# An adaLN transformer block: the LayerNorm chains of the pairs on GpSimd instead of VectorE and ScalarE, with new step orders

## The reference

```
h = layernorm(x) * (1 + ca) + sa
x = x + ga * attention(h)          # causal, softmax over |q k| / 16, then the product with Wo
h = layernorm(x) * (1 + cb) + sb
x = x + gb * ffn(h)
ffn: route each row: scores against 8 cluster and 64 tile signatures go through a
     piecewise linear curve, argmax cluster, argmax tile inside it; gelu/tanh compress to 2 numbers;
     the chosen tile's small spline gives a magnitude; y = h + magnitude * direction[tile] * scale;
     result = layernorm(y) * gamma + beta
```

## Time and profile before

| | |
|---|---|
| median of 3 runs | 475.73 us |
| profiled execution, its own time | 474.78 us |
| its span (first to last instruction) | 473.0 us |
| busy: PE, DVE, ACT, POOL | 403.7, 400.6, 295.5, 42.7 us |
| granted TensorE clock, mean | 0.939 |

### The profile page before, as it was taken

The page is one execution under the profiler, slowest core; times in us unless marked ns, Lnnn a source line. Parts: engine busy times, 40 slices in busy tenths (PEclk is TensorE's granted clock), DMA queues, the critical chain, the costliest instruction groups (busy, mean ns, idle before and its releaser), DMA issues.

```text
span 473.0 us, 7756 instructions
## 1 busy us (share of the span) xinstructions
PE 403.7 (85%) x2136; PEld 315.1 (67%) x2136; DVE 400.6 (85%) x1367; ACT 295.5 (62%) x645; POOL 42.7 (9%) x64
## 2 busy tenths in 40 slices
PE   2595799999999998999899989998999999963330
PEld 2563568767886886779586858786878787863330
DVE  4436536478799999999999999999999989998986
ACT  2230274949885968597758776797669865772410
POOL 2000003000000022001300040004000400040040
PEclk9879799999999999999999999999999999987565
DMA  8602102100300051104210320024101100110022
GB/s 303 148 2 79 48 1 62 41 11 2 100 2 33 8 161 46 34 2 135 77 35 1 122 91 35 1 59 154 24 1 49 65 24 1 67 46 0 0 90 89
DMA packets 26206, 26.59 MB, mean 56 GB/s; under 512 B 3874, under 2 KB 23588, under 8 KB 26164
## 3 DMA queue, kind: packets, MB, share of 16 engines
q1 hardware_dynamic: 24132, 24.25, 16.1%
q10 hardware_dynamic: 2032, 1.85, 1.2%
HBM read 17.66 MB, written 8.44 MB: 55 GB/s over the span
## 4 chain that ended last, share of the span: by engine, by line
DVE 51%; PE 32%; issue 9%; ACT 4%; ACTq 2%; DVEq 0%
PE bank L476 6%; PE bank L495 6%; PE bank L466 4%; PE bank L453 4%; PE bank L518 3%; DVE x L1043 3%; DVE res L1240 3%; DVE st L998 3%; DVE seg_val L1099 3%; DVE st L1206 3%; DVE val L1102 3%; DVE y L1230 3%; DVE v L1022 3%; DVE probs L1029 3%; DVE st L1049 2%
## 5 line engine op out<-in xcount | busy, mean ns | idle before, releaser
L476 PE MATMUL bank<-h,g 128*128 128x128 f32 (+3 forms) x256 | 80.6, 444 | 8.1 <-DVE v L1022 8.1
L495 PE MATMUL bank<-v,probsT 128*128 128x257 f32 x320 | 80.5, 383 | 0.0
L934 POOL TENSOR_TENSOR res<-x,gb_row 128x512 f32<-128x512 f32 x32 | 40.3, 1279 | 413.7 <-DMA out<-res 339.7
L466 PE MATMUL bank<-m_sb,h 128*128 128x258 f32 x256 | 66.0, 382 | 0.0
L476 PEld LDWEIGHTS bank<-h,g 128*128 128x128 f32 x256 | 44.5, 195 | 27.5 <-issue 11.0
L495 PEld LDWEIGHTS bank<-v,probsT 128*128 128x128 f32 x320 | 56.8, 190 | 8.0 <-issue 1.3
L453 PE MATMUL bank<-h,a_sb 128*128 128x512 f32 x128 | 59.8, 596 | 1.5 <-ACT gath L788 1.4
L466 PEld LDWEIGHTS bank<-m_sb,h 128*128 128x128 f32 x256 | 44.6, 192 | 6.8 <-issue 2.2
L699 ACT ACTIVATE bank<-bank,v 128x128 f32<-128x128 f32 (+1 forms) x64 | 31.6, 494 | 26.8 <-PE bank L476 23.8
L674 ACT ACTIVATE xhat<-x,nmr,rstd 128x256 f32<-128x256 f32 x64 | 36.7, 594 | 15.7 <-DVE nmr L989 15.7
L1029 DVE CUSTOM_DVE_ANT_0 probs<-bank,cmask 128x128 f32<-128x128 f32 (+1 forms) x64 | 31.1, 485 | 12.7 <-ACT bank L699 12.7
(11 more groups left out here) (175 smaller groups left out, 769.7 us busy)
## 6 DMA issues: line engine op xcount, KB each, us to landing
x<-in_L_attn_x SPq DMA_DIRECT2D x16, 512.0 KB, 3.8
out<-res SPq DMA_DIRECT2D x16, 512.0 KB, 3.0
gb_row<-gate_rows SPq DMA_DIRECT2D x16, 256.0 KB, 3.1
ga_row<-gate_rows SPq DMA_DIRECT2D x16, 128.0 KB, 2.9
wide<-in_L_wmod ACTq DMA_DIRECT2D x2, 768.0 KB, 7.3
res<-in_L_attn_Wq SPq DMA_DIRECT2D x1, 256.0 KB, 4.9
res<-in_L_attn_Wk SPq DMA_DIRECT2D x1, 256.0 KB, 7.2
res<-in_L_attn_Wo SPq DMA_DIRECT2D x1, 256.0 KB, 9.8
```

Of the source, the lines that this page charges most:

```text
L466: last = mm(ps[:, 0:VW], h[s][:, c, t * P:(t + 1) * P], m_sb[:, c, :], start=False, stop=(c == KC - 1))
L476: last = mm(ps[:, 0:w], g[s][:, c, t * P:(t + 1) * P], h[s][:, c, 0:w], start=(c == 0), stop=(c == KC - 1))
L495: last = mm(ps[:, 0:D + 1], probsT[s][t][:, j * P:(j + 1) * P], v_sb[s][:, j, 0:D + 1], start=(j == 0), stop=(j == t))
L934: gp.tensor_tensor(res[:, 2 * u:2 * u + 2, :], x2[p % 2][s][:, t, :], gb_row[p % 2][s][:, 1:2, :].broadcast_to([P, 2, D]), ALU.add).then_i ...
```

## The change

The three chains of the pairs go to GpSimd, as one step each: `a_ln`, `c_ln`, `y_ln`. The steps `a_var`, `a_nw`, `c_var`, `c_nw`, `y_var`, `y_nw` on DVE and `a_gs`, `c_gs`, `y_gs` on ACT are gone; the two halves of pair 0's LN1 in the setup stay as they were. The new chain has 14 operations, most of which wait for the one before; 1/sqrt is a `pow` with exponent -0.5, followed by a Newton step. `oa` now waits for the whole LN3 chain.

```diff
+            def layer_norm(chain, ln, ready):
+                ...
+                chain.mark(tt(dif, st[:, :, 1], st[:, :, 4], ALU.subtract))
+                chain.mark(tt(sums, st[:, :, 1], st[:, :, 4], ALU.add))
+                chain.link(pool, tt(var, st[:, :, 2], st[:, :, 5], ALU.add))
+                chain.mark(ts(var, var, 1.0 / D, EPS, ALU.mult, ALU.add))
+                chain.link(pool, tt(dif, dif, dif, ALU.mult))
+                chain.mark(ts(dif, dif, 0.25, None, ALU.mult))
+                chain.link(pool, ts(nmu, sums, -0.5, None, ALU.mult))
+                chain.link(pool, tt(var, var, dif, ALU.add))
+                chain.link(pool, tt(rstd, var, neg_half[:, :], ALU.pow))
+                chain.link(pool, tt(newt, rstd, rstd, ALU.mult))
+                chain.link(pool, tt(newt, newt, var, ALU.mult))
+                chain.link(pool, ts(newt, newt, -0.5, 1.5, ALU.mult, ALU.add))
+                chain.link(pool, tt(rstd, rstd, newt, ALU.mult))
+                tt(nmr, nmu, rstd, ALU.mult).then_inc(ready, 1)
+            @step
+            def a_ln(p):
+                pool_ln1.at(p - 1)
+                pool.wait_ge(st1_rdy, PT * p)
+                need(pool, xhat_ready, PT * p)
+                layer_norm(pool_ln1, ln1, ln1_ready)
+            @step
+            def c_ln(p):
+                pool.wait_ge(st2_rdy, PT * (p + 1))
+                ...
+            @step
+            def y_ln(p):
+                pool.wait_ge(st3_rdy, PT * (p + 1))
+                ...
             def superstep(k):
-                for i in range(0, 4):
-                    base(k, i)
-            for k in range(0, PAIRS + 0):
+                y_ln(k - 4)
+                base(k - 3, 0)
+                a_ln(k)
+                for i in range(1, 4):
+                    base(k - 3, i)
+                c_ln(k - 1)
+            for k in range(0, PAIRS + 4):
                 superstep(k)
...
             def oa(p, t):
                 if t == 0:
-                    dve_ln3.at(p)
-                    dve_ln3.wait(dve)
+                    dve.wait_ge(ln3_ready, p + 1)
```

More of the change, by code:

```diff
@@ L816, in _ @@
             first_half(1)
-            ahead.add(("a_gs", 0, ()))
             act.wait_ge(bias_rdy, 1)
@@ L1404, in superstep @@
-                a_st(k, 0, 3)
+                    y_st(k - 4, i)
+                b_ttr(k - 1, 0, 0)
+                for i in range(9, 12):
+                    loc(k - 3, i)
+                a_st(k, 0, 3)
+                a_st(k, 1, 0)
+                c_b2(k - 3)
+                for i in range(0, 2):
+                    lob(k - 3, i)
+                oa(k - 4, 0)
+                b_v(k - 1, 0, 1)
+                lob(k - 3, 2)
+                oa(k - 4, 1)
+                b_v(k - 1, 0, 2)
@@ new lines, in superstep @@
+                ob(k - 4, 5)
+                a_st(k, 1, 2)
+                b_ttr(k - 1, 0, 2)
+                oa(k - 4, 7)
+                ob(k - 4, 6)
+                b_v(k - 1, 1, 0)
+                ob(k - 4, 7)
+                clc(k - 2, 0)
+                a_st(k, 1, 3)
+                for i in range(1, 10):
+                    clc(k - 2, i)
+                spl(k - 3, 0)
+                b_ri(k - 1, 0, 0)
+                clc(k - 2, 10)
+                b_v(k - 1, 1, 1)
+                spl(k - 3, 1)
@@ new lines, in superstep @@
+                clc(k - 2, 11)
+                spl(k - 3, 2)
+                clb(k - 2, 0)
+                spl(k - 3, 3)
+                b_ttr(k - 1, 0, 3)
+                clb(k - 2, 1)
+                spl(k - 3, 4)
+                b_x2(k - 1, 0, 0)
+                clb(k - 2, 2)
+                spl(k - 3, 5)
+                b_v(k - 1, 1, 2)
+                clb(k - 2, 3)
+                y_(k - 3, 0)
+                clb(k - 2, 4)
+                y_(k - 3, 1)
+                b_ttr(k - 1, 1, 0)
@@ L1405, in superstep @@
+                pick(k - 2, 0)
+                y_st(k - 3, 0)
+                pick(k - 2, 1)
+                b_ttr(k - 1, 1, 1)
+                y_(k - 3, 2)
+                b_ri(k - 1, 0, 1)
+                b_x2(k - 1, 0, 1)
+                y_(k - 3, 3)
+                loc(k - 2, 0)
+                y_st(k - 3, 1)
+                loc(k - 2, 1)
+                b_ttr(k - 1, 1, 2)
                 y_(k - 3, 4)
-                y_st(k - 3, 0)
+                loc(k - 2, 2)
+                b_st(k - 1, 0, 0)
@@ L1468, in superstep @@
-                b_ttr(k - 1, 1, 0)
-                for i in range(7, 9):
-                    loc(k - 2, i)
-                b_ri(k - 1, 0, 1)
-                loc(k - 2, 9)
-                y_nw(k - 3, 1)
-                loc(k - 2, 10)
-                b_ttr(k - 1, 1, 1)
-                loc(k - 2, 11)
-                c_b2(k - 2)
-                lob(k - 2, 0)
+                loc(k - 2, 3)
+                b_v(k - 1, 1, 3)
+                y_st(k - 3, 2)
+                b_st(k - 1, 0, 1)
@@ new lines, in superstep @@
+                loc(k - 2, 4)
+                b_ri(k - 1, 0, 2)
+                b_x2(k - 1, 0, 2)
+                y_st(k - 3, 3)
+                loc(k - 2, 5)
+                y_st(k - 3, 4)
+                b_ttr(k - 1, 1, 3)
+                b_st(k - 1, 0, 2)
+                b_ri(k - 1, 0, 3)
+                b_ri(k - 1, 1, 0)
+                b_x2(k - 1, 0, 3)
+                b_st(k - 1, 0, 3)
+                b_ri(k - 1, 1, 1)
+                for i in range(0, 2):
+                    b_x2(k - 1, 1, i)
```

481 lines of the change are left out of this document (201 added, 280 removed), and 16 rows, old and new, of the table BANK.

## The result

The changed kernel took 575.18 us, median of 6 runs (574.19 to 579.35), against 475.0 us, median of 6 runs of the kernel before (measured again beside it): 1.2122 times as long, 95% interval [1.2082, 1.2163]. Forecast were 480.5 us, range 468 to 492. The direction was right and the size wrong by 95 us.

What follows compares the result with a forecast made beforehand. DVE was taken to bound the full pipeline, PE 2.7 us behind. Ramp -4.2, four periods -6.0, pair 7's step -2.1 and drain +18 made +5.7 us on the profiled execution's 474.78: 480.5 us, range 468 to 492.

Steps and rivals of the forecast that it cites:

- their term of the sum: Full pipeline: four periods, each going from 49.3 to 47.8 us, were to give -6.0 us.
- the match of 43.9 us: DVE work left in a full-pipeline period: 49.3 us less 3.3 of chain work and 2.1 of stall.
- The price of a chain: One norm's chain of 14 small operations on GpSimd: 3.5 us, with bounds of 2.2 and 17.5 us.
- rival 3: A dear chain: 6 us each on GpSimd, waited for twice per period, giving 508 us; chance 0.13.
- the prediction's own sign: Prediction wrong if drain is under 68 us, period at 46.6, or a GpSimd chain takes 5 us and more.
- a wait of 0.5 us: Full pipeline, LN3: DVE reaches oa at 7.6 us, y_ln ends at 8.1, so DVE waits 0.5 us.
- a wait of 2.0 us on DVE: Full pipeline, LN1: spl needs c_ga, held on ACT behind a_xh and a_ln, so DVE waits 2.0 us.
- PE's work per pair doesn't change: TensorE's work in each pair was to stay at 46.6 us, the floor of the period.
- The ramp: Start to last b_x2 of pair 2: reordered PE work 3.2 us and earlier first scores about 1 us, -4.2 us.
- pair 7's step: Step of pair 7, without a_st: 44.0 us with stalls against 46.1 before, -2.1 us.
- the drain: Last b_x2 to the end: +18 us, from more DVE work left, chain waits and bases.
- 1.8 + 1.4 + 3.5 = 6.7: Drain: DVE's waits before oa for y_ln, two of 1.8 and 1.4 us and the last of 3.5.

Runs made afterwards that it cites:

- e7: Kernel before with one line added: the first two GpSimd bases of a pair also wait for the second send; 466.2 us, 0.980 of before.
- e5: Changed kernel with each GpSimd chain cut from 14 operations to three, all new orders kept; 481.7 us.
- e10: Changed kernel with ScalarE's first c_xh moved behind b_g, b_abs and first GELUs, and first a_xh behind b_pt, c_ga and b_g; 528.5 us.
- e13: Kernel before with bases later and all three norms' chains on GpSimd (third's -mean on VectorE), second norm's ahead of the bases; 476.5 us.

## Why the prediction was wrong

- **What bounds the kernel before: right.** DVE with a stall of 2.1 us beside GpSimd's bases, PE 2.7 us behind. e7 removed that stall alone and the period fell by 2.0 us to 47.2. (The mean of the four periods is 49.15 us and not 49.3, so their term of the sum is -5.4 and not -6.0.)
- **What the change takes away: right in size, and the match of 43.9 us partly luck.** DVE is busy 44.0 to 44.3 us in a period. But the 43.9 are 5.4 taken from the period of 49.3; taken from DVE's busy 47.9 us they leave 42.5, to which the prediction adds 2.5 of stalls beside GpSimd (0.9 - 0.3 + 1.2 + 0.7). Like set against like, 45.0 were forecast.
- **The price of a chain: the first term that was mis-sized.** 3.5 us were taken, 5.1 to 6.5 measured. A link is 0.28 us and not 0.23; the pow 1.67 us, for which I had allowed a few tenths; and up to 1.5 us of meeting wide DVE operations. The bounds of 2.2 and 17.5 us held it, but rival 3, which says "6 us", had a chance of 0.13 only. The nearest row by size, a memset, says nothing of a pow. By the prediction's own sign, a chain of 5 us and more, it is refuted.
- **The waits: the step that failed.** The prediction has "a wait of 0.5 us" for LN3, "a wait of 2.0 us on DVE" for LN1 and none for LN2. For LN2 I missed that `c_ln`'s reader is ACT: `c_xh(k-1,0)` in front of `b_g(k,0,1)` is in the new ACT order and PE hangs on `b_g`. It cost 4.0 us of ACT and 3.3 of PE per period. For LN1 I saw that ACT holds `b_pt` and `c_ga` behind `a_xh`, but priced what DVE waits, 2.0 us, where 4.7 were measured, and not that PE hangs on `b_pt`, 5.0 us. The wait of 0.5 for LN3 did not come in the full pipeline. That rival 3 gave 508 us with about the right chain and two waits a period tells the same: even at the true length the waits, with the clock behind them, were 67 us short. e5 is the converse: with chains of 0.66 us, where the missed wait vanishes, the kernel takes 481.7 us.
- **"PE's work per pair doesn't change": failed.** Its matmuls don't, its time does: 47.1 to 52.9 us, since in most periods a stretch of 6.8 us at half clock begins behind the one idle and another within the other. The earlier trace rows has the granted clock at 1.00 in the full pipeline and 0.65 in the drain, so the column was there to read. The prediction holds no term for it; by the estimate above it was worth nearly half of what a period grew.
- **The parts of the sum.** The ramp: forecast -4.2, measured +29.4; four periods: -6.0, measured +46.3; pair 7's step: -2.1, measured +6.7; the drain: +18, measured +21.7 (79.2 us against the 75.5 that were worked out). Only the drain came near, and that was partly luck. DVE waits for a chain three times in it:

```profile
509.84 0.48 DVE L1254 SCALAR_TENSOR_TENSOR y<-y,nmu,gb_row 128x256 f32<-128x256 f32 x1 [6.09 <-POOL nmr L971]
...
542.21 0.48 DVE L1254 SCALAR_TENSOR_TENSOR y<-y,nmu,gb_row 128x256 f32<-128x256 f32 x1 [3.10 <-POOL nmr L971]
...
567.23 0.88 DVE L1254 SCALAR_TENSOR_TENSOR y<-y,nmu,gb_row 128x256 f32<-128x256 f32 x2 [5.17 <-POOL nmr L971]
```

  These are 14.4 us where 1.8 + 1.4 + 3.5 = 6.7 were forecast, while the new orders by themselves cost 7.7 (e5) and not the 12 of DVE's work and the bases: two errors that nearly cancel. In e5 the ramp is 3.1 us earlier than before, so most of the -4.2 for the reordered PE work was sound and lay under the waits. Of the full pipeline's gain nothing shows even there: 49.0 us a period, pair 7's step the same as before.
- **The port rule.** The operations of two SBUF operands that met the bases took 1.28 us, and `var` on GpSimd 1.15 instead of 0.20 us when DVE's `seg_val` of 1.08 us was under way: the blocking goes both ways. The Trainium skill, page "SBUF — State Buffer", section "SBUF: two separate sides", calls it an exclusive lock held for a whole instruction; the trace agrees. It was the smaller part: 1.0 us of `c_ln`, 1.5 of `a_ln`.

What stays open: how the 94 us divide exactly between the wait itself and the clock. The period of the kernel after splits into 6.4 us more idle and 5.8 us slower matmuls, and the one period with the same waits and one stretch at half clock fewer, 58.6 us, bears that out for one stretch; none had the same waits and no such stretch. Why the clock stayed up behind that one idle of 3.3 us is open too. And e10's last 4 us a period over e5 are read from its waits and not tested.

## What to carry to other kernels

Before a chain is moved to another engine, list every reader of its result, and on each reader's in-order engine what stands behind the waiting instruction: two waits of 4 to 5 us per pair on ScalarE stood in a kernel 21% slower than before, though the engine that was relieved had been the bound, and setting other work in front of them gave 47 of the 100 us back. The same holds for the engine that takes the chain in: exchanging two steps in GpSimd's queue was worth 64 us. And look first for the cheap form of the gain: DVE's stall, 2.0 of the 2.7 us that stood between DVE and PE in a period, went by starting two operations 6 us later, which is one line and 2% faster than before.

## What the hardware showed that I had not expected

- `pow` on GpSimd with two tensor operands takes 1.67 us for 8 elements per lane (x23, mean 1666 ns); multiply, add and subtract of that size take 0.20 us, and 0.28 us from start to start when one waits for the other, so that 14 of them all linked would take 3.8 us without any pow. On DVE linked operations of this size start 0.20 us apart (`dif` at 222.58 and `var` at 222.78 in e7).
- Short idles of TensorE can cost clock: one of 3.3 us (265.9 to 269.2) was followed by 6.8 us at the 1.2 GHz level from 270.2 on, in a pipeline that otherwise ran at 2.4 GHz. It isn't so each time: behind the idle of 3.3 us that ended at 210.6 the clock stayed at 1.00. In e13, where PE is idle for 0.6 us at that place, the granted clock is 1.00 from 150 to 420 us.
- GpSimd's `base` operations (two SBUF operands) beside DVE's `y_`, which reads one operand in PSUM, and beside bn_stats, with one operand, slowed neither: 1.25 us each for four, 0.42 us for a `y_`.
